# A fused two-block transformer layer on one core: q's and k's weights also loaded turned for the Gram products, and split in two parts of columns

## The reference

```
x = x + tanh(g_xattn[0]) * cross_attention(layernorm(x), ctx)    # 16 heads of 128, q and k with RMS norm
x = x + tanh(g_ffn[0])   * mixture_of_lora(layernorm(x))         # 8 experts, the best 2
x = x + tanh(g_xattn[1]) * batched_attention(layernorm(x), ctx)  # sigmoid scores
x = x + tanh(g_ffn[1])   * expert_mlp(layernorm(x))              # 8 experts, the best 1
```

```
q = rms_norm(x @ q_w + q_b);  k = rms_norm(ctx @ ki_w + ki_b);  v = ctx @ vi_w + vi_b
scores = q @ k.T / sqrt(128) per head;  out = softmax(scores) @ v;  return out @ o_w + o_b
```

## Time and profile before

| | |
|---|---|
| median of 3 runs | 1311.98 us (1311.91 to 1312.0) |
| profiled execution | 1310.84 us, its span 1309.0 us |
| PE busy | 1294.2 us (99%) |
| DVE busy | 765.1 us (58%) |
| ACT busy | 727.3 us (56%) |
| POOL busy | 67.7 us (5%) |
| transfers | 108.44 MB, mean 83 GB/s |
| transfers in the first 38 us | 285 GB/s |

### The profile page before, as it was taken

The page is one execution under the profiler, slowest core; times in us unless marked ns, Lnnn a source line. Parts: engine busy times, 40 slices in busy tenths (PEclk is TensorE's granted clock), DMA queues, the critical chain, the costliest instruction groups (busy, mean ns, idle before and its releaser), DMA issues.

```text
span 1309.0 us, 26268 instructions
## 1 busy us (share of the span) xinstructions
PE 1294.2 (99%) x10249; PEld 1143.4 (87%) x10249; DVE 765.1 (58%) x2309; ACT 727.3 (56%) x2037; POOL 67.7 (5%) x112
## 2 busy tenths in 40 slices
PE   8999999999999999999999999999999999999998
PEld 8889889988998889988899888998889988898887
DVE  7645656646565565655556465564656646564585
ACT  4365756556465564655545655546646556556522
POOL 0000000000000000010000100001000000001010
PEclk9999999999999999999999999999999999999999
DMA  8221441132222231223212232123312112212101
GB/s 323 105 97 49 150 142 65 46 101 97 66 65 81 77 102 66 65 66 129 74 41 81 66 113 81 49 66 98 111 51 82 49 66 97 66 51 78 50 1 49
DMA packets 42985, 108.44 MB, mean 83 GB/s; under 512 B 3696, under 2 KB 22384, under 8 KB 42096
## 3 DMA queue, kind: packets, MB, share of 16 engines
q1 hardware_dynamic: 42864, 106.77, 24.1%
HBM read 94.17 MB, written 12.58 MB: 82 GB/s over the span
## 4 chain that ended last, share of the span: by engine, by line
PE 92%; DVE 4%; ACT 2%; issue 1%; DMA 1%; SPq 0%; DVEq 0%; ACTq 0%
PE bank L116 63%; PE bank L1022 8%; PE bank L1032 5%; PE bank L991 3%; PE bank L1132 2%; PE bank L1144 2%; PE bank L1011 2%; PE bank L1086 1%; PE bank L970 1%; PE bank L1176 1%; ACT logit L734 1%; DMA raw<-in_L_xattn_q_w_dram 1%; PE bank L998 0%; PE bank L1153 0%; DVE wt L1461 0%
## 5 line engine op out<-in xcount | busy, mean ns | idle before, releaser
L734 ACT ACTIVATE logit<-logit,least 128x64 f32<-128x64 f32 x512 | 171.1, 337 | 180.5 <-DVE least L1569 180.5
L116 PE MATMUL bank<-sv,ct_hi 128*128 128x256 f32 x1024 | 195.8, 290 | 0.0
L116 PE MATMUL bank<-so,ao_hi 128*128 128x256 f32 x1008 | 193.8, 291 | 0.1
L116 PEld LDWEIGHTS bank<-sv,ct_hi 128*128 128x128 f32 x1024 | 158.2, 188 | 13.1 <-issue 10.7
L116 PEld LDWEIGHTS bank<-so,ao_hi 128*128 128x128 f32 x1008 | 153.4, 188 | 7.8 <-issue 7.6
L1022 PEld LDWEIGHTS bank<-pt,v_sb 128*128 128x128 f32 x1024 | 133.7, 191 | 11.3 <-ACT pt L742 0.3
L116 PE MATMUL bank<-sv,ct_lo 128*128 128x256 f32 x512 | 142.8, 279 | 0.0
L752 ACT ACTIVATE v_sb<-bank 128x512 f32<-128x512 f32 x128 | 76.1, 594 | 119.6 <-PE bank L116 119.6
L116 PE MATMUL bank<-so,ao_lo 128*128 128x256 f32 x504 | 140.5, 279 | 0.0
L1557 DVE SCALAR_TENSOR_TENSOR ao_lo<-bank,vecs,ao_hi 128x512 fp32r<-128x512 f32 x126 | 94.6, 751 | 76.7 <-ACT ao_hi L728 76.5
L1022 PE MATMUL bank<-pt,v_sb 128*128 128x128 f32 x1024 | 134.8, 274 | 0.1
(11 more groups left out here) (235 smaller groups left out, 2518.4 us busy)
## 6 DMA issues: line engine op xcount, KB each, us to landing
sv<-v_scratch SPq DMA_DIRECT2D x56, 512.0 KB, 3.4
so<-o_scratch SPq DMA_DIRECT2D x56, 512.0 KB, 3.3
xin<-in_x_dram SPq DMA_DIRECT2D x8, 512.0 KB, 4.5
cin<-in_ctx_pairs_dram SPq DMA_DIRECT2D x8, 512.0 KB, 5.8
cs<-in_ctx_turned_dram SPq DMA_DIRECT2D x8, 512.0 KB, 4.6
xres<-in_x_dram SPq DMA_DIRECT2D x8, 512.0 KB, 4.8
v_scratch<-sv SPq DMA_DIRECT2D x8, 512.0 KB, 2.8
o_scratch<-so SPq DMA_DIRECT2D x8, 512.0 KB, 2.8
```

The lines of the kernel that those rows point to most:

```text
L116: last = pe.matmul(out, lhs[a], rhs[b], start=start and n == 0, stop=stop and n == 2, **kw)
L734: last = act.activation(logit[:, h % 2, t, :], logit[:, h % 2, t, :], ACT.Exp, scale=-1.0, bias=least[:, h % 2, t:t + 1], accum_out=rsum[: ...
```

## The change

Two new inputs, `turned_q` and `turned_k`, hold the weights of q and k with the bias as a 257th row, already turned (128 x 16 x 257). They are loaded in four quarters each to `wt_q` and `wt_k`; the transposes and copies are gone. `wt_k` lies where `sv` and `so` are later, so the first high part of v waits for k's Gram matrix. The raw weights are still loaded, now into the place of the low parts, and in two parts of columns: 512 (heads 0 to 3) and 1536. Only the first parts are split before the steps. k's later high parts stand ahead of ScalarE's step 0 and q's behind it, k's later low parts stand behind VectorE's steps 1 and 2, q's behind step 3.

```diff
+FIRST_HEADS = 4
+PARTS = (slice(0, FIRST_HEADS * HD), slice(FIRST_HEADS * HD, INNER))
+WEIGHT_PARTS = [(n, c, part) for part in range(2) for n in "kq" for c in range(DC)]
...
-        sp.dma_start(raw[0][:, 0:INNER // 2], q_w[0:P, 0:INNER // 2]).then_inc(s_first, 16)
         sp.dma_start(vecs[:, :], columns).then_inc(s_vec, 16)
-        sp.dma_start(raw[0][:, INNER // 2:], q_w[0:P, INNER // 2:]).then_inc(s_raw[0], 16)
-        sp.dma_start(raw[1][:, :], q_w[P:2 * P, :]).then_inc(s_raw[1], 16)
-        load_inputs(0)
+        load_turned_weights("q")
+        sp.dma_start(xin[:, :, :], view(x_t, 0)).then_inc(xin_in.sem, 16)
+        load_turned_weights("k")
+        load_weights("k", 0)
         load_turned(0)
-        for c in range(DC):
-            sp.dma_start(raw[2 + c][:, :], ki_w[c * P:(c + 1) * P, :]).then_inc(s_raw[2 + c], 16)
-        sp.dma_start(vraw[:, :, :], vi_w.rearrange("(c p) n -> p c n", p=P)).then_inc(s_vraw, 16)
+        load_weights("q", 0)
+        sp.dma_start(cin[:, :, :], ctx_pairs[0]).then_inc(cin_in.sem, 16)
+        load_value_weights(0)
+        load_weights("k", 1)
+        load_weights("q", 1)
+        load_value_weights(1)
...
         def gram_matrix(n, f):
 
-            pe.wait_ge(s_prepev, 1 + 10 * n + TURN_BANKS + f + 1)
+            wt, dst = (wt_q, GRAM_BANKS[0]) if n == "q" else (wt_k, GRAM_BANKS[1])
+            pe.wait_ge(s_wt[n][f], 16)
...
         for f in range(4):
-            turn_weight(0, 0, f)
-        turn_weight(0, 1, 0)
-        for f in range(4):
-            if f < 3:
-                turn_weight(0, 1, f + 1)
-            gram_matrix(0, f)
+            gram_matrix("q", f)
+        gram_matrix("k", 0)
+        gram_matrix("k", 1)
         transposes(-1, 0)
-        for f in range(4):
-            turn_weight(1, 0, f)
         transposes(-1, 1)
...
+        gram_matrix("k", 2)
+        gram_matrix("k", 3)
         project(0, 0, 0)
...
         split_context(0)
         split_tokens(0)
+        high_parts("q", 0)
         value_high(0)
+        high_parts("k", 1)
+        step(0, 0)
         value_high(1)
+        high_parts("q", 1)
...
         for h in range(H):
             step(0, h)
+            if h in (1, 2):
+                low_part("k", h - 1, 1)
+            if h == 3:
+                for c in range(DC):
+                    low_part("q", c, 1)
```

More of the change, by code:

```diff
@@ L169, in layers @@
     w_hi = {n: sb(f"{n}_hi", [P, DC, INNER], F32R) for n in "qk"}
+    with ExitStack() as early:
+        raw = {n: early.enter_context(nc.sbuf_tensor(f"raw_{n}", [P, DC, INNER], F32)) for n in "qk"}
     w_lo = {n: sb(f"{n}_lo", [P, DC, INNER], F32R) for n in "qk"}
+    with ExitStack() as early:
+        wt_k = early.enter_context(nc.sbuf_tensor("wt_k", [P, H, D + 1], F32))
     sv = sb("sv", [P, 2, 2, DC, 2 * HD], F32R)
     so = sb("so", [P, 2, 2, 2, D], F32R)
+    sb("so_end", [P, H], F32)
     with ExitStack() as early:
@@ L277, in layers @@
     s_tanh = sem("s_tanh")
-    s_raw = [sem(f"s_raw{i}") for i in range(4)]
-    s_first = sem("s_first")
+    s_raw = {(n, c, part): sem(f"s_raw_{n}{c}_{part}") for n in "qk" for c in range(DC) for part in range(2)}
+    s_wt = {n: [sem(f"s_wt_{n}{f}") for f in range(4)] for n in "qk"}
     s_whi = sem("s_whi")
@@ L285, in layers @@
     s_chain = sem("s_chain")
-    s_vraw = sem("s_vraw")
+    s_vraw = [sem(f"s_vraw{part}") for part in range(2)]
     s_oraw = sem("s_oraw")
@@ L681, in _, with high_parts @@
     def _(act):
[L682 to L687, removed]
+        def high_parts(n, part):
+            for c in range(DC):
+                act.wait_ge(s_raw[n, c, part], 16)
+                act.activation(w_hi[n][:, c, PARTS[part]], raw[n][:, c, PARTS[part]], ACT.Copy).then_inc(s_whi, 1)
         def value_high(p):
             if p == 0:
-                act.wait_ge(s_vraw, 16)
+                act.wait_ge(s_vraw[0], 16)
+                act.wait_ge(s_prep, GRAMS_MADE)
+            if p == 2:
+                act.wait_ge(s_vraw[1], 16)
             if p >= 2:
@@ L925, in _ @@
         act.activation(tg[:, :], tg[:, :], ACT.Tanh).then_inc(s_tanh, 1)
-        for h in range(H):
+        for h in range(1, H):
             step(0, h)
@@ L947, in _ @@
     def _(pe):
[L948 to L963, removed]
         def gram_matrix(n, f):
-            pe.wait_ge(s_prepev, 1 + 10 * n + TURN_BANKS + f + 1)
+            wt, dst = (wt_q, GRAM_BANKS[0]) if n == "q" else (wt_k, GRAM_BANKS[1])
+            pe.wait_ge(s_wt[n][f], 16)
             for c in range(DC):
                 for h in range(4 * f, 4 * f + 4):
-                    last = pe.matmul(banks[TURN_BANKS + c][:, c * P:D + 1], wt[:, h, c * P:(c + 1) * P],
+                    last = pe.matmul(banks[dst[c]][:, c * P:D + 1], wt[:, h, c * P:(c + 1) * P],
                                      wt[:, h, c * P:D + 1], start=h == 0, stop=h == H - 1)
@@ L1397, in _ @@
         pe.wait_ge(s_chain, BSQ_READY)
-        pe.matmul(banks[TURN_BANKS + 1][:, 0:2 * H], ones[:, :], bsq[:, :, :].rearrange("p n h -> p (n h)"),
+        pe.matmul(banks[BETA_BANK][:, 0:2 * H], ones[:, :], bsq[:, :, :].rearrange("p n h -> p (n h)"),
                   start=True, stop=True).then_inc(s_prep, 1)
@@ L1933, in _ @@
         gram_copies(1)
-        gram_sums(0, 0)
-        gram_sums(0, 1)
+        for c in range(DC):
+            low_part("q", c, 0)
         value_low(0)
-        gram_sums(0, 2)
-        gram_sums(0, 3)
+        for t in range(NT):
+            gram_sums(0, t)
         square_norms(0)
@@ L1983, in laid_out, with turned_weights @@
         a["L1_ffn_Bw"].transpose(0, 2, 1).reshape(CT1, P, D).transpose(1, 0, 2).reshape(P, CT1 * D)], 1)
-    return {"ctx_pairs": ctx, "ctx_turned": turned, "columns": columns, "later": later}
+    def turned_weights(n):
+        with_bias = np.concatenate([a[f"L0_xattn_{n}_w"], a[f"L0_xattn_{n}_b"][None]], 0)
+        return with_bias.reshape(D + 1, H, HD).transpose(2, 1, 0)
+    return {"ctx_pairs": ctx, "ctx_turned": turned, "columns": columns, "later": later,
+            "turned_q": turned_weights("q"), "turned_k": turned_weights("ki")}
 def build(nc, a, out):
```

82 lines of the change are left out of this document (29 added, 53 removed).

## The result

The changed kernel takes 1314.05 us (median of 19 runs, 1313.19 to 1315.76) against 1311.91 us for the kernel before in the same session (19 runs, 1310.73 to 1313.69): ratio 1.0017, 95% interval 1.0010 to 1.0024. That is 2.1 us slower, inside the 0.2% that the prediction counted as no change, and 0.5 us from its 1314.6. The profiled execution took 1313.46 us, against a sum of 1313.4. The total hides that two terms of the prediction were too large, and that a loss which it did not have made up for them.

A forecast was written before the change was run, and what follows sets the result against it. TensorE, busy 1294.2 of 1309.0 us, was taken as the bound, with VectorE's list a second clock early on. Terms +0.1 and +2.5 us gave 1313.4 us for the profiled execution, 1314.6 as median; range 1309.6 to 1316.8.

The forecast's parts named there:

- TensorE's part: In the preparation: 64 transposes go, the first k projection starts 9.5 us earlier, the Gram sums end near 36.5 us.
- The transfers: In the load queue: `oraw` lands at 46.6 us, the second group's `xin` behind it at 48.0; VectorE waits 4 us.
- Rival 2: The queue empties earlier, `xin` lands by 44 us (faster from a landing before 45.3), time 1308.1 us; chance 0.12.
- rival 3: Weight rows of 4112 bytes load slower, up to 4 us, middle +2, with the clock down: 1316.6 us; chance 0.12.
- VectorE's list: VectorE from the second group's statistics to the first `logit`: 4.4 us plus 1.7 for k's low part, `logit` at 54.1.
- the first term: At the first `logit`, in the first steps: it comes 1.2 us earlier than before, so -1.2 us.
- The pause and the clock: Before 57.1 us TensorE idles 5.6 us, the granted clock falls under 1.00 behind it: +2.5 us.
- rival 1: The clock holds through TensorE's idle stretch: same transfers, +0.1 us, 1312.1 us, range 1311.0 to 1313.4; chance 0.30.
- the sum: Whole kernel: +0.1 + 2.5 = +2.6 us on the profiled execution's 1310.84 us, giving 1313.4 us.
- q's low parts: Behind step 3 they take VectorE 3.4 us, make `logit` 1.5 us late and cost TensorE 1.3 us.
- rival without a clock term: Same as rival 1: TensorE's idle stretch costs no clock, +0.1 us, 1312.1 us; chance 0.30.

The follow-up runs named there:

- The kernel kept awake: The changed kernel with 20 matmuls of ones, read by nobody, added in TensorE's idle stretch of step 2: 1312.06 us, ratio 1.0004 to the kernel before.

## Why the prediction came out where it did

**TensorE's part: right.** The first k projection was forecast for 28.8 us and started at 27.89; the Gram sums for 36.5, and `xin` was issued behind them at 35.76. The 10 us gained were handed back.

**The transfers: right in mechanism, 1.1 us late in size.** `oraw` was to land at 46.6 and landed at 45.5, the second `xin` behind it at 48.0 and 46.93; VectorE waited 4.5 us for it, forecast 4. That these agree is in part luck: VectorE was also free 1.4 us earlier than forecast (42.55 against 43.9). The cut of `oraw` shows the cause by taking it away: the wait vanished, and the time fell by 4.9 us. Rival 2 is out, since it needed a landing before 45.3. So is rival 3: the first piece of `wt_k` was issued at 3.56 and took 8.3 us, the `xin` ahead of it was issued at 3.06 and took 7.5, so a piece with rows of 4112 bytes landed 1.3 us behind its forerunner, the price of rows of 4096 (a piece is 514 KB as the trace counts; the prediction's 526 are thousands of bytes).

```profile
wt_k<-in_turned_k_dram SPq DMA_DIRECT2D x1, 514.0 KB, 8.3
xin<-in_x_dram SPq DMA_DIRECT2D x1, 512.0 KB, 7.5
```

**VectorE's list: right.** From the statistics to the first `logit`, with k's low part, it took 6.1 us, forecast 4.4 + 1.7. So the first term is -2.2 us at TensorE (56.09 against 58.30), forecast -1.2, all of the difference from the landing.

**The pause and the clock: right in kind, too dear.** The pause was 5.55 us, forecast 5.6. The clock fell, to 0.50, and rival 1 with it. No run shows the 2.5 us that the sum has for it: the low level began inside the pause, where no work stood, and the 3.47 us of work at 0.50 come to an estimated 1.7 us. Keeping TensorE busy gave back 1.84 us.

**q's low parts: about right.** From 73.10 to 74.04 there are 0.94 us; with -2.2 and +1.7 that leaves 1.4 for them, forecast 1.3. The kernel kept awake, where no clock term enters, says 1.56. Moving them gained only 1.1 in the medians, since the pause grew.

**What was missing.** These terms sum to +0.94, not +2.6. The step that failed is the second sentence on the bound: "later on both kernels issue the same work, so what counts is how much later or earlier TensorE gets there". Both issue the same work, but on buffers 64 bytes higher, and that cost 1.65 us over the rest of the span. The line that moved them, `sb("so_end", [P, H], F32)`, is part of the change, though the excerpt of the diff leaves it out: it reserves 64 bytes because `wt_k` is that much longer than `sv` and `so` together. With 512 bytes in its place the changed kernel takes 1312.51 us, close to the 1312.1 that the prediction gave to its rival without a clock term, though the clock was low there too (0.50 from 54 to 60 us). The forecast fell within 0.5 us by luck: an overestimate of 1.7 us and an omission of the same size met.

## What to carry to other kernels

Read a diff for what it does to addresses as well as to instructions: an allocation that no instruction names can move every later operand, and where TensorE is busy for 98% of the span 2 ns more in two kinds of matmul (281 against 279) went with 1.8 us. Before the work in front of a bound is shortened, ask what the next input's transfer will then stand behind; here a 2 MB load of which a quarter was wanted soon, cut in two with that input in between, gave 4.9 us. Put new work of an engine where it already waits for another, not where the others wait for it, and look at what else runs there (beside GpSimd's addition a low part took 2.29 us in place of 1.75); and check a total that comes out right against positions in the middle of the trace.

## What the hardware showed that I had not expected

- With every buffer behind `so` 64 or 128 bytes higher, the kernel before lost 1.8 and 2.8 us of 1311 between step 4 and the last matmul (`so,ao_lo` 281 against 279 ns in both, `sv,ct_lo` 281 and 280); with 256 bytes it lost 0.0, and with 512 the changed kernel 0.1 (both products at 279).
- The clock's low level began 2.2 us into the pause in the changed kernel and some 4.2 us into it with q's low parts moved (TensorE's work of 0.49 us from 50.00 on, low from 54.72), and lasted 6.8 us in both, 3.47 and 4.73 us of it with work under way. Half of that work, 1.7 us and 2.4, is my estimate of the price. A pause of 3.60 us, in the kernel with the cut load, left it at 1.00 in the profile, but two of that kernel's 11 runs have the 0.997 of a run with a low stretch.
- It also fell without a long pause. In the profiles with 64 bytes, and with 64 bytes ahead of `ao` only, TensorE waits in the preparation for q's weights, 0.80 and 1.43 us (0.73 and 1.48) with 1.09 us of work between, then 0.35 for VectorE after as much work, and the clock is 0.50 from 12.1 to 15.4 us (12.2 to 15.6), all of it under work. Half of that, 1.7 us, is my estimate of the price; those profiles have lost 2.4 us by step 4. The two profiles of the kernel before have one such wait for q's weights, 0.75 and 0.64 us, and 1.00 throughout. The profile with 256 bytes has longer ones, 1.54 and 1.48 us, again with 1.09 us of work between and 0.35 for VectorE behind, and reads 1.00 throughout too: what sets the level there is not shown.
- At the start the weight loads take 333 ns, against 187 later for the same shape, while the granted clock reads 1.00 from 0 us on.
- VectorE's subtraction over 1536 columns was slower where it ran beside GpSimd's addition to `xres`, and not where transfers alone ran. It took 1.75 us with the low part ahead of the tanh, where transfers ran at 360 GB/s and GpSimd was idle (41.09 to 42.84). It took 2.29 in the kernel with the cut load, where GpSimd's addition ended 0.7 us into it, and 2.16 each as a pair with GpSimd at work throughout. There the addition slowed too, to 5.88 us in place of 2.85 in the changed kernel. No run moves the addition by itself, so this rests on the four traces. The addition beside q's low parts, whose 4.31 us from 43.53 stand above:

```profile
43.25 5.88 POOL L671 TENSOR_TENSOR xres<-xres,obias 128x256 f32<-128x256 f32 x4 [40.93 <-DVE obias L1921]
```
